# Two mixture-of-experts stages: rows gathered by token lists instead of scattered into slots

## The reference

```python
logits = x @ router                    # layer 1: 16 experts, layer 2: 8, layer 3: 7
vals, idx = top_k(logits, 2)           # weights w: softmax of the two, or normalised probabilities
out = sum_k w[:, k] * expert[idx[:, k]](x)
# layer 1: relu, 256 wide; layer 2: gelu, 512 wide, both with biases
# layer 3: silu(x @ gate) * (x @ up), 512 wide, plus one shared expert for every token
```

## Time and profile before

| | us |
|---|---|
| median of 3 runs | 1220.57 (1219.39 to 1220.91) |
| profiled execution | 1218.35 |
| its span | 1216.7 |
| TensorE busy | 972.5 (80%) |
| VectorE busy | 844.3 (69%) |
| POOL busy | 565.4 (46%) |
| ScalarE busy | 534.2 (44%) |
| mean granted TensorE clock | 0.916 |

### The profile page before, as it was taken

How to read it: one execution, slowest core, us unless ns; L and a number is a source line. 1 busy time by engine, 2 the same in 40 slices (tenths; PEclk the granted TensorE clock), 3 DMA queues, 4 the chain that set the end, 5 groups by cost and what they waited for, 6 DMA issues and landing times. The chain is left out here.

```text
span 1216.7 us, 29907 instructions
## 1 busy us (share of the span) xinstructions
PE 972.5 (80%) x12222; PEld 699.0 (57%) x12232; DVE 844.3 (69%) x1508; ACT 534.2 (44%) x1334; POOL 565.4 (46%) x390
## 2 busy tenths in 40 slices
PE   6648778878889989998283898796796899857795
PEld 2237667667676555555273466454595566523795
DVE  6589999999996975587432796697223799754243
ACT  5634444444451843562142482284162788312121
POOL 3299999999985703111455310211543422003232
PEclk9859999999999999999597999999697999977898
DMA  3568889888968000000483000000672000005682
GB/s 121 132 189 223 217 229 233 229 234 227 227 179 307 2 1 1 1 2 1 120 238 117 1 2 1 1 2 1 225 252 93 1 2 2 1 1 185 219 303 73
DMA packets 74903, 139.81 MB, mean 115 GB/s; under 512 B 8544, under 2 KB 28912, under 8 KB 74544
## 3 DMA queue, kind: packets, MB, share of 16 engines
q1 hardware_dynamic: 70800, 129.72, 36.9%
q0 software_dynamic: 3968, 8.18, 1.9%
HBM read 128.04 MB, written 14.82 MB: 117 GB/s over the span
## 5 line engine op out<-in xcount | busy, mean ns | idle before, releaser
L936 ACT ACTIVATE shifted_a<-scores,nmax_a 128x128 f32<-128x128 f32 x768 | 207.8, 401 | 34.0 <-DVE nmax_a L870 28.9
L1588 ACT ACTIVATE decay<-decay 128x1016 f32<-128x1016 f32 x128 | 123.9, 1002 | 150.1 <-PE decay L1473 150.1
L373 POOL TENSOR_TENSOR rstd<-ve,neghalf 128x4 f32<-128x4 f32 x30 | 31.5, 1050 | 240.3 <-DVE ve L358 240.3
L1473 PE MATMUL decay<-delta,A_pairs 32*128 32x127 f32 x2048 | 82.6, 303 | 71.2 <-DVE small_pack L1632 33.6
L870 DVE TENSOR_REDUCE nmax_a<-scores 128x4 f32<-128x512 f32 x192 | 123.0, 684 | 16.5 <-PE scores L753 15.4
L877 DVE COPY PTs_a<-PT 128x512 f32<-128x512 f32 x192 | 124.3, 682 | 9.8 <-PE PT L766 9.5
L1473 PEld LDWEIGHTS decay<-delta,A_pairs 32*128 32x128 f32 x2048 | 69.8, 204 | 90.0 <-DVE small_pack L1632 39.5
L1930 POOL DMA_INDIRECT results<-xs_s x76 | 72.7, 956 | 104.3 <-DVE xs_s L2105 96.6
L766 PE MATMUL PT<-mamba_pack,shifted_a 128*128 128x128 f32 x768 | 117.6, 277 | 0.0
L766 PEld LDWEIGHTS PT<-mamba_pack,shifted_a 128*128 128x128 f32 x768 | 88.4, 141 | 22.7 <-issue 8.0
L1140 POOL TENSOR_TENSOR pos_bias<-pos_bias,B 128x1024 f32<-128x1024 f32 x37 | 88.3, 2408 | 5.9 <-DMA pos_bias<-du_rows 3.3
(11 more groups left out here) (485 smaller groups left out, 2251.4 us busy)
## 6 DMA issues: line engine op xcount, KB each, us to landing
pos_bias<-du_rows SPq DMA_DIRECT2D x74, 256.0 KB, 4.9
small_pack<-L3f_w SPq DMA_DIRECT2D x15, 768.0 KB, 4.9
O<-du_rows SPq DMA_DIRECT2D x38, 256.0 KB, 4.7
masked_cos<-du_rows SPq DMA_DIRECT2D x36, 256.0 KB, 4.8
masked_sin<-du_rows SPq DMA_DIRECT2D x36, 256.0 KB, 5.0
XN<-du_rows SPq DMA_DIRECT2D x36, 256.0 KB, 5.0
XNT<-du_rows SPq DMA_DIRECT2D x36, 256.0 KB, 4.9
small_pack<-L2f_w SPq DMA_DIRECT2D x15, 514.0 KB, 5.2
```

The costliest lines, as they stand in the source:

```text
L373: nc.gpsimd.tensor_tensor(rstd[:, bs], ve[:, bs], m.neghalf[:, bs], ALU.pow).then_inc(m.rstd_ready, 1)
L936: t = nc.scalar.activation(shifted[u % 4][:, j, :], scores[u % 5][:, j, :], ACT.Exp, scale=-1.0, bias=nmax[:, u % 5, j:j + 1])
L1473: t = nc.tensor.matmul(decay[(2 * p + side) % DEEP][:, s, i, 1:S], A_pairs[strip, c, 8 * q + 2 * i:8 * q + 2 * i + 2, :].rearrange("p j n ...
L1588: nc.scalar.activation(x, x, ACT.Exp, scale=-1.0).then_inc(decayed, 1)
```

## The change

In layers 2 and 3 the rows aren't scattered any more. SP stores all tokens to DRAM at the stage's start (`tokens`). VectorE splits each slot into its block and its place in it; TensorE multiplies the marks of the places with the marks of the blocks, scaled by the batch index, the partition and the choice, and so inverts the list: for each slot of each block, the token that it takes (`Listing`). POOL then fetches each block's rows with one indirect DMA by that list, 23 in layer 2 and 22 in layer 3, on 8 semaphores in turn. The numbers of the result rows are worked out from the same product, later, and POOL's scatters of the results use them.

The first group of four blocks becomes four groups of one in layer 2, and one of one and one of three in layer 3. In layer 3 only one shared unit goes ahead of the ranking, and the shared units have an order of their own: ScalarE copies the up product and the activated gate product out (`held`), and VectorE multiplies them later. In layer 2 TensorE gets 10 and 6 filling products in place of the 14. The context's products move from layer 2 to the end of layer 1's stage, behind its blocks. In all three layers a row no longer carries its weight: VectorE copies a block's result, and weighs it in the sum into `X`, with one step per 128x128 piece. The initial fills of layer 2's and layer 3's slots go. Layer 1 keeps its scatters.

```diff
-ROW = D + 2
+ROW = D + 1
+GATHERED = {"L1f": 0, "L2f": 23, "L3f": 22}
+COLLECTED = ()
+SCATTERED = [layer for layer in BLOCKS if GATHERED[layer] < BLOCKS[layer]]
...
-            for layer in ("L1f", "L2f", "L3f"):
+            for layer in SCATTERED:
...
+class Listing:
+    def split(self, dve, slot, steps):
+        steps.done(dve, nc.vector.tensor_scalar(self.ahead[:], slot[:], -63.75, 1.0 / 128.0, ALU.add, ALU.mult))
+        steps.done(dve, nc.vector.tensor_scalar(self.ahead[:], self.ahead[:], ROUND, None, ALU.add))
+        steps.done(dve, nc.vector.tensor_scalar(self.block_of[:], self.ahead[:], -ROUND, None, ALU.add))
+        nc.vector.tensor_tensor(self.in_block[:], bcast_mid(m.w("iota128")[:, 0:n], 16), bcast_last(self.block_of[:], n),
+                                ALU.is_equal).then_inc(self.blocks_known.sem, self.blocks_known.by(1))
+        steps.done(dve, nc.vector.scalar_tensor_tensor(out=self.place_in[:], in0=self.block_of[:], scalar=-128.0,
+                                                       in1=slot[:], op0=ALU.mult, op1=ALU.add))
...
+        for g in range(16):
+            t = nc.vector.tensor_scalar(self.at_place[:, g, :], self.iotab[:], self.place_in[:, g:g + 1], None,
+                                        ALU.is_equal)
...
+    def invert(self, pe):
+        pe.wait_ge(self.lows_scaled.sem, self.lows_scaled.at(1))
+        pe.wait_ge(self.batches_scaled.sem, self.batches_scaled.at(1))
+        for g in range(16):
+            if g % 4 == 0:
+                pe.wait_ge(self.places_known.sem, self.places_known.at(g // 4 + 1))
+            t = self.nc.tensor.matmul(self.ps, self.at_place[:, g, :], self.scaled[:, g, :, :].rearrange("p x j -> p (x j)"),
+                                      start=(g == 0), stop=(g == 15))
...
+    def number_sources(self, dve, steps):
+        dve.wait_ge(self.inverted.sem, self.inverted.at(1))
...
+        nc.vector.tensor_copy(self.source_i[:], self.source[:]).then_inc(self.sources_ready.sem, self.sources_ready.by(1))
...
+    if DIRECT:
+        GROUPS = [range(0, 1), range(1, 4)] + GROUPS[1:] if gated else [range(j, j + 1) for j in range(4)] + GROUPS[1:]
...
             if gated:
                 sp.dma_start(shared[:], weights[E]).then_inc(shared_loaded.sem, shared_loaded.by(16))
+            if DIRECT:
+                sp.dma_start(m.dram["tokens"].rearrange("(b t) d -> t b d", t=S), source[:]
+                             ).then_inc(rows_stored.sem, rows_stored.by(16))
             sp.wait_ge(listed.sem, listed.at(1))
...
+            def gather(j):
+                done = gathered[j % GATHERS]
+                if j >= GATHERS:
+                    pool.wait_ge(done.sem, done.at(16 * (j // GATHERS)))
+                nc.gpsimd.indirect_dma_start(xs[:, j, 0:D], None, m.dram["tokens"],
+                                             bass.IndirectOffsetOnAxis(ap=listing.source_i[:, j:j + 1], axis=0)
+                                             ).then_inc(done.sem, done.by(16))
+            if DIRECT:
+                listing.set_constants(pool)
+                listing.scale_batches(pool)
+                pool.wait_ge(rows_stored.sem, rows_stored.at(16))
+                pool.wait_ge(listing.sources_ready.sem, listing.sources_ready.at(1))
+                for j in range(DIRECT):
+                    gather(j)
...
-                for u in range(UPS):
-                    shared_up(u)
+                shared_up(0)
             pe.wait_ge(steps.sem, route.onehot_value)
...
             if gated:
-                for u in range(UPS, 2 * FC):
+                for u in range(1, len(shared_units)):
                     shared_up(u)
+                if DIRECT:
+                    listing.invert(pe)
                 for half in range(2):
                     shared_to_down(half)
             else:
+                if DIRECT:
+                    keep_awake(10)
+                    listing.invert(pe)
                 pe.wait_ge(comb_ready.sem, comb_ready.at(1))
...
+                if DIRECT:
+                    keep_awake(6)
                 pe.wait_ge(begun.sem, begun.at(2))
-                if context is not None:
-                    context.products(pe)
-                    context.wait_copied(pe)
...
+            if transforms:
+                pe.wait_ge(acted.sem, acted.at(NB))
+                pe.wait_ge(y_copied.sem, y_copied.at(NB))
+                context.products(pe)
...
+                for u, (half, fc) in enumerate(shared_units):
+                    if u == 6 and DIRECT:
+                        listing.scale_lows(act)
+                    act.wait_ge(shared_up_done.sem, shared_up_done.at(u + 1))
+                    nc.scalar.activation(shared_hid[half][:, fc, :], U[u % UPS][:], ACT.Copy)
+                    nc.scalar.activation(held[u], G[u % UPS][:], func).then_inc(shared_taken.sem, shared_taken.by(1))
...
+            if DIRECT:
+                listing.split(dve, slot, steps)
             steps.done(dve, nc.vector.tensor_tensor(past[:], bcast_last(m.w("iota128")[0:1, 0:NB], EP),
...
+            if DIRECT:
+                listing.number_sources(dve, steps)
...
+            for u in range(len(shared_units) if gated else 0):
...
+                dve.wait_ge(shared_taken.sem, shared_taken.at(u + 1))
+                nc.vector.tensor_tensor(x, x, held[u], ALU.mult).then_inc(shared_gated.sem, shared_gated.by(1))
...
-            def weigh(j):
+            def copy_y(j):
                 dve.wait_ge(downed.sem, downed.at(j + 1))
-                nc.vector.tensor_scalar(xs[:, j, 0:D], Y[j % 2][:, 0:D], xs[:, j, D + 1:D + 2], None,
-                                        ALU.mult).then_inc(y_weighed.sem, y_weighed.by(1))
+                nc.vector.tensor_copy(xs[:, j, 0:D], Y[j % 2][:, 0:D]).then_inc(y_copied.sem, y_copied.by(1))
...
         def combine(dve, half):
...
-            x = m.X[:, halves[half], :]
-            steps.done(dve, nc.vector.tensor_tensor(x, x, back[:, 0, halves[half], :], ALU.add))
-            nc.vector.tensor_tensor(x, x, back[:, 1, halves[half], :], ALU.add).then_inc(combined.sem, combined.by(1))
+            for k in range(2):
+                for b in range(halves[half].start, halves[half].stop):
+                    t = nc.vector.scalar_tensor_tensor(out=m.X[:, b, :], in0=back[:, k, b, :],
+                                                       scalar=route.wt[:, b, k:k + 1], in1=m.X[:, b, :],
+                                                       op0=ALU.mult, op1=ALU.add)
...
```

More of the change, by code:

```diff
@@ L1814, in sparse_stage @@
     XTS = 3
-    BESIDE = 2 * FC if gated else 0
+    COLLECT = layer in COLLECTED
+    results = m.dram[f"slots_{layer}"] if COLLECT else m.dram["results"][0:2 * T + NB * 128, :]
     N = EP * 16
-    slots = m.dram[f"slots_{layer}"]
-    results = m.dram["results"][0:2 * T + NB * 128, :]
+    slots = m.dram[f"slots_{layer}"] if DIRECT < NB else None
     with ExitStack() as ctx:
@@ L1843, in sparse_stage @@
             shared_hid = [m.pos_bias[:].rearrange("p (c x) s -> p c (x s)", c=FC), sb("shared_hid", [128, FC, HALF])[:]]
-            shared_loaded, shared_down = sem("shared_loaded"), sem("shared_down")
+            shared_loaded, shared_up_done, shared_taken, shared_gated, shared_down = (
+                sem(f"shared_{n}") for n in ("loaded", "up_done", "taken", "gated", "down"))
+            shared_units = [(half, fc) for half in range(2) for fc in range(FC)]
+            held = [back[:, k, 4 * i:4 * i + 4, :].rearrange("p b d -> p (b d)") for k in range(2) for i in range(2)]
+            held += [h[:].rearrange("p c s -> p (c s)") for h in hid] + [silu[0][:]]
         else:
@@ L1868, in sparse_stage @@
         cols = lambda half: slice(half * HALF, (half + 1) * HALF)
+        column = lambda j: slice((j - GROUPS[group[j]][0]) * 128, (j - GROUPS[group[j]][0] + 1) * 128)
         block = ctx.enter_context(nc.Block())
@@ new lines, in _ @@
+            if DIRECT:
[5 more added lines that the diff above has]
+                    gather(j)
+            if DIRECT < NB:
+                nc.gpsimd.tensor_copy(rows_out[:, :, :, D].bitcast(I32),
+                                      m.w("numbers").rearrange("p (k b) -> p k b", k=2)
+                                      ).then_inc(numbered.sem, numbered.by(1))
+                pool.wait_ge(m.slots_set, 16 * len(SCATTERED))
+                pool.wait_ge(numbered.sem, numbered.at(1))
+                pool.wait_ge(copied_out.sem, copied_out.at(2))
+                pool.wait_ge(placed.sem, placed.at(1))
+                for b in range(B):
+                    for k in range(2):
+                        g = k * B + b
+                        done = scattered if b < 6 else last_scattered
+                        nc.gpsimd.indirect_dma_start(slots, bass.IndirectOffsetOnAxis(ap=slot_i[:, g:g + 1], axis=0),
+                                                     rows_out[:, k, b, :], None).then_inc(done.sem, done.by(16))
@@ new lines, in _ @@
+            if COLLECT:
```

(34 more changed lines are left out.)

252 lines of the change are left out of this document (172 added, 80 removed).

## The result

The kernel after takes 1215.26 us (median of 20 executions, 1203.29 to 1224.28), the kernel before 1219.93 on the same chips; the ratio is 0.9938, 95% interval 0.992 to 0.9956, so the change gains 7.6 us (5.4 to 9.8). Forecast was 11.2, at 1209.4. The ratio leaves out the two slow executions of the 20, and the profiled one, at 1223.22, is one of these two.

What follows compares the result with a forecast made beforehand. Chains of waits bound the stages: POOL's scatters largest in layer 3, POOL's queue last in layer 2. Layer 2 9.5, layer 3 6.3, sums -4.3, small -0.4 and +0.1 make 11.2 off 1220.57: 1209.4, range 1204.5 to 1216.

Steps and rivals of the forecast that it cites:

- The list in layer 2: Layer 2, VectorE's added steps before POOL's release: sum 6.85 less 0.3, first gather at 860.35 instead of 853.80.
- POOL's queue: Layer 2: 23 gathers and 23 results scatters at pitch 1.26, POOL ending at 918.05 against 927.62, 9.5 gained.
- rivals 2 and 3: Gathers cheaper than scatters, at 0.96: 1202.5, chance 0.05; gathers dearer on POOL, gain gone at pitch 1.75: chance 0.10.
- TensorE does not set this end: Layer 2's end: TensorE's last result near 911, when POOL still has 4 or 5 scatters to do.
- Layer 3: Layer 3's stage: ranking 2.9 earlier, TensorE gap 3.2 before the down products, block 0 near 1133, 6.3 us gained.
- I take it that it falls: Layer 3: TensorE's clock falls to half in the gap before the shared down products, 2.9 us lost.
- rival 1: Layer 3: TensorE's clock holds over the gap, 2.9 us more gained, 1206.5; chance 0.20.
- Rival 4: List early but rows land late, under the weight loads; 1212 at landings of 12 us; chance 0.10 with rival 5's slower VectorE steps.
- The sums: Every stage's end: weights applied in the sum, 2.4 against 1.4 per half, costing 4.3 us in all (2.5 to 6).
- The context products: After layer 1's blocks: end by 660.9, about with POOL's last scatter, costing nothing; without that cover 11.
- The rule weighed: Layer 2: VectorE's comparisons lock POOL's scalings out, inversion up to 1 us later, sum 10.2.
- Whatever VectorE does beside them: POOL's results scatters take 952 to 962 ns regardless of VectorE's work at the same time.

Runs made afterwards that it cites:

- `groups_of_four`: Changed kernel with layer 2's first blocks turned and copied four at a time again, instead of singly; 1211.31 us in one execution.
- `best`: Changed kernel plus earlier layer 3 inversion, second group's copy before block 0's gate, later tokens' store, earlier layer 2 row numbers, more filling products; 0.9893 of the kernel before.
- `gating_first`: Changed kernel with layer 3's four gating products of the first half ahead of the row numbers on VectorE; 0.9917 of the kernel before.
- `neither`: Changed kernel with layers 2 and 3 both scattering their rows as before, the rest of the change kept; 1.0034 of the kernel before.
- `l3_only`: Changed kernel with layer 2 scattering its rows as before, layer 3 still fetching by the list; 0.9985 of the kernel before.

## Why the prediction was right, point by point

- **The list in layer 2**: first gather 6.55 later forecast, 875.75 against 859.73 is 16.02 after the router products, 9.78 before: 6.24. Block comparison 0.54 as priced, 16 comparisons 3.24 (3.4).
- **POOL's queue**: 46 pieces at 1.25 to 1.27, the first apart (1.26). Its end, 918.05 by the forecast, is 74.0 after the stage's start; measured 73.9 to 74.1 where TensorE's clock rose early. Gathers are neither cheaper nor dearer: rivals 2 and 3 fall.
- **"TensorE does not set this end"** is the step that failed, in three of the profiles. Block 0 came as said (23.8; forecast 23). But "the last block's start took 41.4 before" was carried over: the first four blocks, single and with 0.6 us stalls at 1.2 GHz, made it 46.3, and POOL ended at 76.1: 2.0 of the 9.5 lost. That is the forecast's own sign of being wrong: TensorE ends the wait ahead of layer 2's last scatters. A term was missing, the clock of the first blocks, which the forecast asked about in layer 3 alone.
- **Layer 3**: net 4.6 forecast (6.3 less 1.3 and 0.4), 6.2 to 7.9 measured (116.5 in `groups_of_four` apart, whose down products took 10.10). Block 0 came 34.8 us after the stage's start, where "near 1133" is 37.7 and before it was 43.1. The inversion took 0.53, not the bound of 1.9. The gap was 3.1 (3.2). "I take it that it falls" came true in four of the seven profiles with this layer 3, and rival 1, that the clock holds, in the other three; what decides it stays open. Where it fell the down products took 1.6 longer (9.05 against 7.42), not 2.9, and at the last copy at most 1.0 of that is left, so rival 1's 2.9 isn't there either. Block 1 stalled 2.0 (1.7). The shared load took 5.14 instead of 4.12, 1.0 for the 0.4 taken. It is not the store: in `best`, where the store waits for it, the load still takes 5.19. It is 4.1 to 4.3 where layer 3 scatters and 4.9 to 6.1 where it gathers; why stays open. Rival 4, rows that land late, ends a wait of layer 3's turns in `gating_first` alone.
- **The sums**: pitch 0.29 (0.30), 2.31 against 1.42 per half (2.4, 1.4). Priced 4.3 (1.5, 1.5, 1.3), the stages show 1.9, 2.0 and 0.8 to 1.3.
- **The context products** at nothing: right as far as the runs can tell. With ScalarE's copies they end at 665.7, and POOL's last scatter in layer 1 starts at 667.1.
- **The rule weighed**: POOL's two scalings ended at 870.62, half a us ahead of the inversion's first product (871.14), so the us that the forecast weighed did not come. But the two engines did block each other, the other way round. The first scaling and the first comparison, the second two, and a later comparison:

```profile
869.67 0.49 POOL L1862 TENSOR_TENSOR scaled_l<-in_block_l,small_pack 128x184 bf16<-128x184 bf16 x1 [6.68 <-DVE in_block_l L1839]
869.71 0.51 DVE L1845 TENSOR_SCALAR at_place_l<-iotab_l,place_in_l 128x128 bf16<-128x128 bf16 x1
...
870.13 0.50 POOL L1862 TENSOR_TENSOR scaled_l<-in_block_l,small_pack 128x184 bf16<-128x184 bf16 x1
870.14 0.53 DVE L1845 TENSOR_SCALAR at_place_l<-iotab_l,place_in_l 128x128 bf16<-128x128 bf16 x1
...
870.59 0.24 DVE L1845 TENSOR_SCALAR at_place_l<-iotab_l,place_in_l 128x128 bf16<-128x128 bf16 x1
```

  Each of the first two comparisons ends 0.05 behind one of POOL's scalings; the 14 others take 0.24, at a pitch of 0.16. All 20 lists in these traces show it. At that pitch throughout the 16 would take 2.7, an estimate, instead of 3.24, so the list comes 0.5 to 0.6 later for it. The Trainium skill (SBUF — State Buffer, Who interferes with whom) says of VectorE's two-port mode that whichever of VectorE and GpSimd issues first gets the shared ports for the whole instruction and the other blocks. The trace agrees, if the comparisons run in that mode, which no view shows: POOL had started 0.04 and 0.01 ahead. The forecast had weighed only the order in which POOL loses; no run changed that order. The Trainium skill's other rule there, that a VectorE instruction with both inputs in SBUF contends with a GpSimd instruction that reads SBUF, shows too: 1.42 instead of 0.96 in `neither`, 1.37 and 1.35 for layer 3's first two gathers in the kernel after. "Whatever VectorE does beside them" was too wide: that work had an input in PSUM.
- **The sum**: net of their sums layer 2 gave 5.5 to 7.8 (8.0 forecast) and layer 3 6.2 to 7.9 (4.6). Layer 1 lost 1.0 to 3.0 (1.4), the kernel after's profile with 3.7 apart, and 1.4 to 6.3 went in the stage between, which no step of the forecast had. So 11.2 became 7.6 by errors of both signs, and that they nearly cancel is luck. The account is only as good as single executions: the loss in the stage between rests on two profiles of the kernel before.

## What to carry to other kernels

A queue freed on one engine hands the end to the next one, and that one's clock then counts: ask for each stage at which clock its first work runs, and fill TensorE ahead of it. When two pieces of work share an engine's queue, ask who waits for each: in layer 3 the gating ahead of the row numbers closed one gap and opened another, and starting the row numbers sooner closed both. When work is moved from PSUM to SBUF operands, look at what POOL does beside it. Compare stages, not ends, when the gain is under 1%: unchanged stages move by as much. And when a stage comes out as forecast, check each cause for itself, as in `best`.

## What the runs showed of the hardware

An indirect DMA from POOL is slowed by a 128x512 VectorE product with both inputs in SBUF: 0.96 becomes up to 1.42, and 2.73 beside three in a row and most of a fourth; beside products with one input in PSUM it stays 0.95 to 0.96 (1.07 for layer 3's first). One gather that was issued 0.01 behind such a product's start took 0.94 all the same (1133.65 in the kernel after), and in `l3_only` the same one took 1.49. A VectorE comparison on bf16 in SBUF that starts behind a POOL product on SBUF ends with it, 0.51 and 0.53 instead of 0.24. Gathers of 128 rows of 512 bytes from DRAM cost POOL 0.94 to 0.97 where nothing slows them (1.11 for layer 2's first) and land, in the kernel after, 2.5 to 8.6 us after issue, beside weight loads. TensorE's granted clock in an unchanged stage fell in one of a few repeating patterns, whose stages differ by up to 6.6 us, and over the same 3.1 us gap in layer 3 it fell in four profiles and held in three.
